# Adding up the eight weighted slots of an edge tile on VectorE: one reduction or three halving additions

## What is computed

```python
e = jnp.einsum('ehd,ehd->eh', k[src], q[dst]) / jnp.sqrt(jnp.float32(H * D))
emax = jax.ops.segment_max(e, dst, num_segments=N)
ex = jnp.exp(e - emax[dst])
denom = jax.ops.segment_sum(ex, dst, num_segments=N)
a = ex / denom[dst]
m = v[src] * a[..., None]
ft2 = jax.ops.segment_sum(m, dst, num_segments=N).reshape(N, F)
```

## Time and profile before

| | us |
|---|---|
| median of 3 runs | 2404.04 |
| lowest, highest | 2401.11, 2412.79 |
| the profiled execution | 2409.18 |
| span of its profile | 2407.3 |
| VectorE busy in the span | 1866.7 (78%) |
| TensorE matmul busy | 1834.8 (76%) |
| ScalarE busy | 1381.1 (57%) |
| POOL busy | 1364.6 (57%) |

### The profile page before, as it was taken

One profiled execution on the slowest core, in us unless ns is written; L12 is line 12 of the kernel. 1 busy time (PEld: TensorE's weight loads), 2 busy tenths in 40 slices (PEclk: granted clock), 3 DMA queues, 4 the chain that ended last, 5 costly groups with the idle time before them and its releaser, 6 DMA issues. The chain is left out here.

```text
span 2407.3 us, 43048 instructions
## 1 busy us (share of the span) xinstructions
PE 1834.8 (76%) x12159; PEld 1279.8 (53%) x12159; DVE 1866.7 (78%) x4076; ACT 1381.1 (57%) x4345; POOL 1364.6 (57%) x1281
## 2 busy tenths in 40 slices
PE   6667777787777588787887871268899849999996
PEld 3322222332322466565665650133688739999996
DVE  6479999999999999999999998635799954444442
ACT  1246666665666376676766664459555426555553
POOL 0077777777777777777777777258100003444442
PEclk9878889888898588888878885579999969999998
DMA  8477777776777777777777777456000182222223
GB/s 235 152 216 210 214 216 210 210 214 202 214 213 211 219 209 224 221 222 229 219 223 220 225 223 222 130 163 175 23 31 30 38 300 46 36 39 35 35 38 74
DMA packets 213154, 395.07 MB, mean 164 GB/s; under 512 B 45987, under 2 KB 140274, under 8 KB 212896
## 3 DMA queue, kind: packets, MB, share of 16 engines
q0 software_dynamic: 91392, 278.99, 41.2%
q1 hardware_dynamic: 98002, 91.87, 12.8%
q10 hardware_dynamic: 23566, 22.00, 2.8%
HBM read 347.29 MB, written 48.65 MB: 164 GB/s over the span
## 5 line engine op out<-in xcount | busy, mean ns | idle before, releaser
L793 POOL DMA_INDIRECT ring<-kv_tab,idx x1008 | 1089.7, 1081 | 422.7 <-issue 413.9
L1110 ACT ACTIVATE val<-ring,val 128x64 f32<-128x64 f32 x2016 | 529.2, 336 | 79.4 <-DVE part L901 75.7
L854 DVE TENSOR_TENSOR prod<-ring,tile_bank 128x1024 f32<-128x1024 f32 x252 | 303.4, 1212 | 75.3 <-DMA ring<-kv_tab,idx 75.0
L861 DVE TENSOR_REDUCE score<-prod 128x16 f32<-128x1024 f32 x252 | 298.5, 1208 | 0.0
L2118 POOL DMA_INDIRECT x_sum<-e_yw,to_row x56 | 124.7, 2227 | 226.0 <-DVE e_yw L2144 210.5
L2103 POOL DMA_INDIRECT xr<-rows,from_row x56 | 55.6, 993 | 291.5 <-issue 287.5
L2193 PE MATMUL e_h<-e_xT,e_now 128*128 128x128 f32 x1792 | 211.2, 277 | 6.3 <-DVE e_now L2134 6.3
L2193 PEld LDWEIGHTS e_h<-e_xT,e_now 128*128 128x128 f32 x1792 | 206.4, 193 | 6.7 <-DVE e_now L2134 6.7
L2208 PE MATMUL e_yps<-e_now,e_hT 128*128 128x256 f32 x896 | 202.5, 379 | 0.0
L2158 ACT ACTIVATE e_now<-e_w_all 128x2048 f32 x56 | 106.9, 1912 | 131.0 <-PE e_yps L2208 131.0
L2208 PEld LDWEIGHTS e_yps<-e_now,e_hT 128*128 128x128 f32 x896 | 166.0, 190 | 20.3
(11 more groups left out here) (416 smaller groups left out, 4643.1 us busy)
## 6 DMA issues: line engine op xcount, KB each, us to landing
loaded<-parts SPq DMA_DIRECT2D x150, 130.0 KB, 2.2
e_w_all<-L_ffn_W SPq DMA_DIRECT2D x16, 1024.0 KB, 12.8
parts<-part ACTq DMA_DIRECT2D x126, 130.0 KB
q_win<-q_tab SPq DMA_DIRECT2D x126, 128.0 KB
ring<-kv_tab,idx POOLq DMA_INDIRECT x1008
kv_tab<-kv_t SPq DMA_DIRECT2D x25, 224.0 KB
xn_buf<-x SPq DMA_DIRECT2D x25, 125.0 KB
xn_buf<-xn_dram SPq DMA_DIRECT2D x5, 625.0 KB
```

The costliest lines, as they stand in the source:

```text
L793: pool.indirect_dma_start(out=ring[:, n % RING, e, :], out_offset=None, in_=t.kv_tab, in_offset=bass.IndirectOffsetOnAxis(ap=idx[n % 6][:, ...
L854: dve.tensor_tensor(prod[half][:, :, :], ring[:, n % RING, at, 0:F], bcast(q_ps[n % 2].unsqueeze(1), 128, L // 2, F), ALU.mult).then_inc(q ...
L861: dve.tensor_reduce(score[:, at, :], prod[half][:, :, :].rearrange("p s (h d) -> p s h d", h=HG), AX.X, ALU.add).then_inc(reduced, 1)
L1110: one = act.activation(val[n % 2][:, e, h, 0:DG], ring[:, n % RING, e, F + h * DG:F + (h + 1) * DG], ACT.Copy, scale=val[n % 2][:, e, h, D ...
```

## The change

The three additions and their two waits on `folding` go, and with them the semaphore. In their place `fold(n)` is one reduction with addition that reads `val` as (numbers, slots), slots innermost, and writes `part`. It stands where the first addition stood, ahead of `compare`, and so do the wait for the store of `part` and the signal `folded`. Reading slots innermost, two numbers that follow each other in the reading lie 260 words apart.

```diff
             def fold(n):
-                v = val[n % 2][:, :, :, :].rearrange("p s h d -> p s (h d)")
                 dve.wait_ge(val_ready, n + 1)
                 dve.wait_ge(act_val_ready, n + 1)
-                dve.tensor_tensor(v[:, 0:4, :], v[:, 0:4, :], v[:, 4:8, :], ALU.add).then_inc(folding, 1)
-
-            def fold_on(n):
-                v = val[n % 2][:, :, :, :].rearrange("p s h d -> p s (h d)")
-                dve.wait_ge(folding, 2 * n + 1)
-                dve.tensor_tensor(v[:, 0:2, :], v[:, 0:2, :], v[:, 2:4, :], ALU.add).then_inc(folding, 1)
-
-            def fold_last(n):
-                v = val[n % 2][:, :, :, :].rearrange("p s h d -> p s (h d)")
-                dve.wait_ge(folding, 2 * n + 2)
                 wait(dve, part_out[n % 3], 16 * (n // 3))
-                dve.tensor_tensor(part[n % 3][:, :], v[:, 0, :], v[:, 1, :], ALU.add).then_inc(folded, 1)
+                dve.tensor_reduce(part[n % 3][:, :], val[n % 2][:, :, :, :].rearrange("p s h d -> p (h d) s"), AX.X, ALU.add
+                                  ).then_inc(folded, 1)
 
             def late(u, kind):
 
@@ -1084,13 +1074,9 @@
                     fold(n - 1)
                 if n + AHEAD + 1 < TILES:
                     compare(n + AHEAD + 1)
-                if old:
-                    fold_on(n - 1)
                 mix(n, 3, 1)
                 if n + AHEAD < TILES:
                     settle(n + AHEAD)
-                if old:
-                    fold_last(n - 1)
                 mix(n, 3, 2)
 
         @block.scalar
```

More of the change, by code:

```diff
@@ L767, in stage_edges_and_mix @@
             s.sem("e_" + n) for n in ("compared", "found", "idx", "spread", "find_read", "placed"))
-        q_ready, q_read, reduced, scored, top_ready, less_ready, exp_ready, val_ready, act_val_ready, folded, folding, sum_ready, part_ready, carrier = (
-            s.sem("e_" + n) for n in ("q", "q_read", "reduced", "scored", "top", "less", "exp", "val", "act_val", "folded", "folding", "sum", "part", "carrier"))
+        q_ready, q_read, reduced, scored, top_ready, less_ready, exp_ready, val_ready, act_val_ready, folded, sum_ready, part_ready, carrier = (
+            s.sem("e_" + n) for n in ("q", "q_read", "reduced", "scored", "top", "less", "exp", "val", "act_val", "folded", "sum", "part", "carrier"))
         level_split, level_in = s.sem("level_split"), s.sem("level_in")
```

## The result

The kernel after takes 2546.32 us (median of 4 runs, 2541.38 to 2547.66), the kernel before 2406.14 us beside it. The ratio is 1.058 with a 95% interval of 1.056 to 1.060: slower by 140 us. The profiled execution of the kernel after took 2547.36 us for a span of 2545.5, 138.2 us above the span before.

What follows compares the result with a forecast made beforehand. POOL was taken to bound the edge stretch, with VectorE just behind. Net VectorE work of +225 us less 73 us of slack gave +152 us, 2556 us on the median; range 2440 to 2640 us.

Steps and rivals of the forecast that it cites:

- What bounds: Edge stretch: POOL, 77% busy, waits for nobody and sets the pace; VectorE, 93% busy, is just behind.
- The removed part: Three additions on VectorE's queue: 2.10 us a tile, where durations would say 2.34 us.
- The 16 us forecast: VectorE's net extra work if the step costs nothing: 0.13 us in each of 126 tiles.
- The added part: Reduction on VectorE: 2080 numbers at 1.84 ns plus 140 ns, 3.97 us, 3.89 on the queue; net +225 us.
- The slack: VectorE's waits behind POOL: 75.0 us for ring and 7.3 for ScalarE, less 9, hide 73 us.
- Put at nothing: Side effects given no cost: earlier part_out wait, settle about 2.1 us later, ScalarE's 75.7 us wait for part about unchanged.
- Rival A: Reduction on VectorE: no penalty for the step, kernel faster by about 50 us, 2354 us; chance 0.13.
- POOL term: POOL's gathers in the edge stretch: 68 us lost beside the removed additions would be regained.
- Signs: Profile after: row about 3.97 us, ring waits near 10 us, VectorE near 99%, POOL waiting for val, long gathers halved.

Runs made afterwards that it cites:

- Experiment 4: The kernel before plus one unused 0.50 us VectorE instruction a tile: one-input reduction 2406.52 us, ratio 1.0007; two-input addition 2413.31 us, ratio 1.0042.
- experiment 3: The kernel after, its reduction reading the 2080 numbers in order (times only): 2360.97 us, 0.982 of the kernel before; 1.021 in a first run.
- experiment 1: The kernel after, its reduction reading val in 14 ways tile by tile, steps of 1 to 260 words and pairs (times only): 2495.5 us in one run.
- experiment 7: The kernel after with slots e and e + 4 beside each other in val, read as even pairs: 2357.83 us, 0.980 of the kernel before.
- experiment 6: The kernel after with val's slots innermost; reduction reads in order, products write with a step of eight words: 2441.83 us, 1.017 of the kernel before.

## Why the prediction was right

The time given was 2556 us, and 2546.32 came; forecast +152, measured +140. The mechanism held in its parts: a dearer reading, less a slack behind POOL.

*What bounds.* That POOL set the pace and VectorE had slack was right against the share of busy time (93 and 77%). Experiment 4 adds 63 us of work to the busier engine, and the time moves by 3 us, within the noise; experiment 3 gives it 8.7 us more and gains 43.

*The removed part.* 2.10 us a tile on the queue, not the 2.34 of the durations. Experiment 3 replaces it by one instruction of 2.31 us, and VectorE's busy time goes up (8.7 us), not down by 3.5 as the durations would have it (291.5 us for 295.0). The 16 us forecast were twice that; the difference, 0.06 us a tile, was not traced.

*The added part.* 3.97 us forecast with 1.84 ns a number, 3.835 came, 1.78 ns. That the row of L872 would do was in part luck. It is for a step of four words, and nothing on hand said that 260 words cost the same; in experiment 1 they do (3860 and 3837 ns), while 26 words cost 4298 ns, 2.00 a number. At that rate the kernel would have come out some 58 us slower (an estimate: 0.46 us more in each of 126 tiles). L2015's 2.09 ns may belong to its step of 25 words in the same way; that step, and a product read so, were not tried. With the queue's share, +225 us were forecast, and +199.6 measured in VectorE's busy time. Of the 25 us between them 17 are the rate (1.84 for 1.78); the rest is, as with the removed part, some 0.07 us a tile, and was not traced.

*The page.* The "Vector Engine (DVE) Microarchitecture Reference" of the Trainium skill, section 5.2, gives 1.73 ns a column for a two-source operation one of whose sources hops 4 KiB at every element, and 2.50 where both sources, or the output alone, step by 24 words. An estimate from the first figure, with the fixed 140 ns, is 3.74 us for this reduction; 3.835 us were measured, 1.78 ns a number. No run here has the second pattern; the nearest, one source with a step of 26 words, cost 2.00. The same section has the full rate only for runs of at least two adjacent words that begin on an 8-byte boundary. Experiment 1 agrees for pairs (2313 ns even, 2982 odd), but not for a step of two words, which has no such runs and took 2314 ns; the measurement decides. The section also remarks that a one-source operation whose reading alternates between two regions 16 KiB apart, writing one word for two read, ran at the full rate. That pattern was not run here. It does not carry over to this reduction, which goes through eight places 1040 bytes apart and paid in full.

*The slack.* 73 us forecast, 67 went. The ring waits gave what they should (75.0 to 4.3 us), but VectorE's wait for ScalarE at `fold` stayed (7.3 to 6.9), where all but the last tile's 2.4 us should have gone. The two errors, -25 and +6, and the 5.7 us behind the edge stage, which no term foresaw, come to -14 us: the span grew by 138.2 us where 152 were forecast. So the errors in part cancel.

*Put at nothing.* ScalarE's wait for `part` was to stay about what it was. It rose from 75.7 us to 131.0. That cost nothing here, for VectorE waits for ScalarE no longer than before, and POOL's waits for `val`, 123.1 us of them for ScalarE, leave VectorE only 4.3 us of ring waits.

*Rival A* was wrong in its condition, no penalty for the step, and right in its number once the condition was made true: 2354 us given, 2361 in experiment 3 and 2358 in experiment 7; the stretch of 1360 us given was 1356.3. Its POOL term was 68 us, measured 66.9. The trace showed this mechanism beforehand. The section "Who interferes with whom" of "SBUF — State Buffer" in the Trainium skill has a VectorE instruction with two SBUF inputs contend with GpSimd's reads, and a reduction never. Experiments 3 and 4 agree in direction. But the same section reports that `tensor_tensor` did not stall DMAs, and infers that descriptor generation needs the shared pair's write interface, which `tensor_tensor` does not take. Here the preparing of a gather was held, up to 2.07 us for 0.946, and the measurement decides.

*Signs.* The row near 3.97, ring waits near 10 (4.3), VectorE near 99% of the stretch (1516.6 of 1545.8, 98%) and POOL waiting for `val` for 1.2 us or more a tile (220 us over 126 tiles, 1.7) came out. The long gathers should have halved; they nearly went, 19 us of loss in place of 136. POOL now often waits for `val` while L882 runs: 61 gathers overlap L882, where 187 did.

## What to carry to other kernels

Count numbers by how they lie, not only how many: on VectorE a float32 number that is read with a step of four words or more cost 1.7 to 2.0 ns here instead of 1.04, and one written with a step of eight about 1.8 (experiment 6, with its caveat). Putting the operands in even pairs, or at a step of two words, took the penalty away. A VectorE instruction with both inputs in SBUF can also make POOL's gathers longer, so replacing it can pay even where VectorE gains nothing. Of two engines that are both nearly full, ask which one never waits for the other; here it set the pace at 77% busy against 93%. Price an instruction by the distance from its start to the next one's: three short ones overlap their neighbours more than one long one.

## What was not expected of the hardware

A step of two words is read (2314 ns) and written (L882, 1219 ns) at the full rate, one of four is not (3860 ns). The penalty is not even: 26 and 52 words cost 4298 and 4171 ns, 20 and 65 words 3676 and 3800. POOL's gathers are held by VectorE's L882, L890 and L895 and pass L854 and the reductions untouched. ScalarE's products of 64 numbers take 61 ns more when they write with a step of eight words, and 5 ns more (341 against 336) with two. And the same program took 2403 us on some chips and 2776 to 2810 us on others, where added work could shorten it.
